# Products of zeros on TensorE: out of the attention loop, into the first maxima

## The chip, the cores and the metric

The kernel runs on one core of a Trainium2 chip. The metric is the device time of the one launch, in microseconds, from the first to the last instruction with what lies around them.

## The reference

One macaron block on `x` of 4 batches x 512 tokens x 128 features: half a mixture-of-experts layer, gated attention with 16 heads of 8 features, and half a mixture-of-experts layer again.

```python
x = x + 0.5 * ffn(layernorm(x), gate_w, Wg, Wu, Wd)      # 8 experts, each takes its 128 best tokens
x = x + attn(layernorm(x), ...)
x = x + 0.5 * ffn(layernorm(x), gate_w, Wg, Wu, Wd)

# attn, for each batch and head
aperture, expression = sigmoid(x @ Wa + ba), sigmoid(x @ We + be)
attn = softmax((x @ Wi) @ (x @ Wo).T / sqrt(8)) * aperture[:, None] * expression[None, :]
attn = attn / (attn.sum(-1) + 1e-8)
out  = rotate_and_scale(attn @ (x @ Wv)) @ Wout
```

The change touches the attention part alone.

## The kernel before

All engines run programs written out by hand and meet at semaphores. The attention part has 16 *steps*: 4 batches by 4 groups `g` of 4 heads. `n` counts them. The queries and keys of a group stand in `q_stack` and `k_stack`, four heads in four blocks of 32 rows, of which a head uses 24 (three parts of its 8 features), and in the scores a 25th row that carries the negative maximum. A step does, for its 4 heads by 4 chunks of 128 tokens:

- 16 units of **maxima**, two steps ahead of use: PE makes a 128 x 512 block of products (`max_scores`, L1120) in one of a ring of three PSUM banks, and DVE reduces it to a negative maximum per row (`take_max`, L794), which raises `max_taken` and so frees the bank. The maxima of a step are turned on PE (`turn_max`, L1128), copied by ACT (L555) and stored as a row of `q_stack` by a DMA of SP.
- 16 units of **scores** in another ring of three banks: PE (`scores`, L1136), then the exponential on ACT (L584) into `probs`.
- 4 **product groups** (`products`, L1150), one for each chunk `c`: four f32 products of `probs` with the values, for the four heads side by side in bank 6, each 2 records in the profile. They wait until ACT has made the chunk's four exponentials. Ahead of the groups of `c` = 1, 2 and 3 stand `KEEP_BUSY` = 6 products of zeros (L1148), 128 rows by 128 columns by 512, f16, which add nothing to bank 6.
- The sums are copied by ACT (L576), turned on PE (`turn_heads`, L1159) and divided on DVE (`norm_heads`, from L860).

PE's order in a step is in `attend`: for `k` = 0 to 7 a unit of scores, one of maxima, one of scores, then what hangs at this `k` (`turn_max` at 0, the last product group of the step before at 1, `turn_heads` at 4, product groups of `c` = 0, 1, 2 at 3, 5, 7), and one of maxima. The last two steps have no maxima; in their place PE turns and projects batches that are done (`turn_combined`, L1220; `project_out`, L1228). Step 0 has no product group at `k` = 1.

Ahead of step 0 the maxima of steps 0 and 1 are made by `first_maxima`, 32 units, with the projections of the last batch between them (`project_qk(3)`, L1087, behind unit 3 of step 0, and `project_vae(3)`, L1100, amid step 1), and in DVE's queue the work that belongs to them; behind the last maxima DVE makes the gates (from L848) before it takes the maxima of step 0's loop.

```python
pe.wait_ge(xnT_ready[1], B)
first_maxima(0, range(RING))
project_qk(3)
first_maxima(0, range(RING, MAX_UNITS))
pe.wait_ge(vae_ready, 2 * 3)
turn_max(0, 0, None)
first_maxima(1, range(MAX_UNITS // 2))
project_vae(3)
first_maxima(1, range(MAX_UNITS // 2, MAX_UNITS))
```

Of the kernel before, what the change touches and what calls it, by code (L numbers as in the profile page):

```python
# [11 lines left out]
P = 128  # L12
# [35 lines left out]
def macaron_block(nc, x_in, Wa, ba, We, be, Wi, Wo, Wv, Wout, chi, beta_p, iv_p, ov_p, gate_w, Wg, Wu, Wd, out):  # L48
# [3 lines left out]
    E, _, I = Wg.shape  # L52
    K = max(1, int(S / E * 2))
    C = S // P
# [12 lines left out]
    with ExitStack() as ctx:  # L67
        def sb(name, shape, dt=F32):
            return ctx.enter_context(nc.sbuf_tensor(name, shape, dt))

        def sem(name):
            return ctx.enter_context(nc.semaphore(name))
# [3 lines left out]
        zeros = sb("zeros", [P, S], F16)  # L76
# [97 lines left out]
        ps = ctx.enter_context(nc.psum_tensor("ps", [P, 8, 512], F32))  # L174
# [53 lines left out]
        max_taken = sem("max_taken")  # L228
# [17 lines left out]

        MAX_UNITS = HG * C
        EXP_UNITS = C * HG
        KEEP_BUSY = 6
        STACK_DMAS = 2 * HG * 16  # L250

        def ring_bank(step, u):


            return (MAX_UNITS * step + u) % RING

        def max_unit(u):

            return u // HG, (u + 2) % HG

        def ring_wait(n, step, u, first_step):


            return n * MAX_UNITS + (u + 1 + (RING - 1 if step == first_step and u == 0 else 0))
# [668 lines left out]
        def _(pe):  # L933
            def chunk(c):
                return slice(c * P, (c + 1) * P)
# [178 lines left out]
            def max_scores(n, step, u):  # L1114

                g = step % G
                qt, j = max_unit(u)
                rows = slice(32 * j, 32 * j + ROWS)
                pe.wait_ge(max_taken, ring_wait(n, step, u, 3))
                nc.tensor.matmul(ps[:, ring_bank(step, u), :], q_stack[rows, g, chunk(qt)], k_stack[rows, g, :],  # L1120
                                 start=True, stop=True).then_inc(max_scores_ready, 1)
# [17 lines left out]
            def products(n, g, c):  # L1139

                pe.wait_ge(probs_ready, n * EXP_UNITS + (HG * c + HG + RING))
                if c == 0:
                    pe.wait_ge(values_ready, 2 * n + 2)
                    pe.wait_ge(heads_copied, n + 1)
                else:

                    for _ in range(KEEP_BUSY):
                        nc.tensor.matmul(ps[:, 6, :], zeros[:, 0:P], zeros[:], start=False, stop=False, skip_group_check=True)  # L1148
                for j in range(HG):
                    last = nc.tensor.matmul(ps[32 * j:32 * j + 32, 6, :], v_ext[:, g, c, j, :], probs[:, c, j, :],  # L1150
                                            start=(c == 0), stop=(c == C - 1), skip_group_check=True)
                last.then_inc(probs_used, 1)

            def turn_heads(n, g, rows):
# [7 lines left out]
            def attend(b, step, first=False, last_batch=False):  # L1162
# [7 lines left out]
                for k in range(MAX_UNITS // 2):  # L1170

                    scores(n, step, 2 * k)
                    if has_max:
                        max_scores(n + 2, step + 2, 2 * k)
                    scores(n, step, 2 * k + 1)
                    if k == 0 and has_next:
                        turn_max(n + 1, (g + 1) % G, None if first else n)
                    if last_batch and step > 1:

                        done = 2 * (step - 2) + k // 4  # L1180
                        if k % 4 == 0 and done < B - 1:
                            turn_combined(done)
                        if k % 4 == 2 and done < B - 1:
                            project_out(done)
                    if k == 1 and not first:
                        products(n - 1, (g - 1) % G, C - 1)
                    if k in (3, 5, 7):
                        products(n, g, k // 2 - 1)
                    if not first and k == TURN_AT:
                        turn_heads(n - 1, g - 1, n + (2 if has_next else 1))  # L1190
                    if has_max:
                        max_scores(n + 2, step + 2, 2 * k + 1)

            def first_maxima(n, units):
                pe.wait_ge(stacks_loaded[n], STACK_DMAS)
                for u in units:
                    max_scores(n, n, u)

            pe.wait_ge(xnT_ready[1], B)
# [8 lines that stand above are left out]
# [23 lines left out]
            for step in range(1, G):  # L1231
                attend(B - 1, step, last_batch=True)
            products(B * G - 1, G - 1, C - 1)
            turn_heads(B * G - 1, G - 1, B * G)
            turn_xn(2, 0)
# [41 lines left out]
```

## Time and profile before

| | |
|---|---|
| median of 3 runs | 559.98 us (557.52 to 560.18) |
| the profiled execution | 560.48 us |
| its span, first to last instruction | 558.8 us |
| mean granted clock of TensorE | 0.931 of full speed |
| PE busy | 456.7 us, 82% of the span |
| DVE busy | 388.1 us, 69% |
| ACT busy | 239.2 us, 43% |
| POOL busy | 56.1 us, 10% |
| DMA, mean over the span | 39 GB/s |

PE's busy time is counted from records of matmuls whose ends are modelled, and weight loads (PEld) run beside them. The granted clock is 1.00 for 2.4 GHz and 0.50 for 1.2 GHz; a stretch that holds a change of the clock shows a value between.

### The profile page before, as it was taken

How to read it: one execution, taken by the hardware profiler on the slowest of the kernel's cores; microseconds unless marked ns; L12 is line 12 of the kernel's file. 1: busy time of each engine (PE TensorE's matmuls, PEld its weight loads, DVE VectorE, ACT ScalarE, POOL GpSimd, SP SyncE). 2: the span in 40 equal slices, each digit the busy share in tenths (PEclk: the TensorE clock that was granted, in tenths of full speed). 3: DMA queues.
4: the chain of work that ended last, by engine and by line, in shares of the span. 5: the costliest groups of instructions: out<-in, count | busy, mean ns of one | idle time of the engine just before them, and what ended most of it. 6: DMA issues, size and time to landing. Idle time of an engine off the chain costs nothing.

```text
span 558.8 us, 8505 instructions
## 1 busy us (share of the span) xinstructions
PE 456.7 (82%) x2540; PEld 225.6 (40%) x2540; DVE 388.1 (69%) x841; ACT 239.2 (43%) x439; POOL 56.1 (10%) x103
## 2 busy tenths in 40 slices
PE   3407999996988989898889898988999711999995
PEld 2402567763443233333233232332343510456773
DVE  6689578878987376766667676766542678948884
ACT  2302533334215355656556565655556210453331
POOL 5700011200001000000000000000000430001210
PEclk9999999998855799999999999999999855899999
DMA  5000011103670110011111000110010000001102
GB/s 153 1 0 1 1 57 56 56 1 113 194 259 1 30 28 19 15 30 29 29 29 28 24 9 25 29 29 1 1 58 1 0 0 2 1 28 58 56 28 75
DMA packets 23146, 21.73 MB, mean 39 GB/s; under 512 B 4113, under 2 KB 16913, under 8 KB 23121
## 3 DMA queue, kind: packets, MB, share of 16 engines
q1 hardware_dynamic: 23120, 21.42, 12.9%
q8 instruction: 13, 0.21, 0.2%
q14 instruction: 13, 0.10, 0.1%
HBM read 13.93 MB, written 7.34 MB: 38 GB/s over the span
## 4 chain that ended last, share of the span: by engine, by line
PE 65%; DVE 20%; issue 11%; ACT 1%; POOL 1%; DMA 1%; DVEq 0%; POOLq 0%; ACTq 0%
PE ps L1148 12%; PE ps L1150 12%; PE ps L1120 11%; DVE neg_max L794 8%; PE ps L1022 4%; DVE probs L733 3%; PE ps L1136 3%; PE ps L1005 2%; PE ps L1037 2%; PE ps L1007 2%; PE ps L1038 2%; PE ps L1006 2%; PE ps L947 2%; PE ps L1159 2%; PE ps L1128 2%
## 5 line engine op out<-in xcount | busy, mean ns | idle before, releaser
L794 DVE TENSOR_REDUCE neg_max<-ps 128x1 f32<-128x512 f32 x256 | 163.4, 684 | 83.3 <-PE ps L1120 83.3
L584 ACT ACTIVATE probs<-ps 128x512 f32<-128x512 f32 x256 | 137.9, 598 | 96.5 <-PE ps L1136 95.5
L1120 PE MATMUL ps<-k_stack,q_stack 24*128 24x512 f32 x256 | 77.2, 537 | 21.0 <-DVE neg_max L794 20.6
L1136 PE MATMUL ps<-q_stack,k_stack 25*128 25x512 f32 x256 | 87.8, 466 | 0.7 <-ACT probs L584 0.7
L1148 PE MATMUL ps<-zeros 128*128 128x512 f16 x288 | 72.9, 391 | 0.0
L1150 PE MATMUL ps<-probs,v_ext 128*32 128x512 f32 x512 | 70.4, 623 | 0.0
L1120 PEld LDWEIGHTS ps<-k_stack,q_stack 24*128 24x128 f32 x256 | 30.0, 196 | 99.1 <-DVE neg_max L794 64.2
L510 ACT CAST picked<-ps 128x512 fp32r<-128x512 f32 x32 | 17.2, 589 | 67.7 <-PE ps L986 67.7
L1148 PEld LDWEIGHTS ps<-zeros 128*128 128x128 f16 x288 | 24.7, 99 | 39.5 <-issue 9.9
L1136 PEld LDWEIGHTS ps<-q_stack,k_stack 25*128 25x128 f32 x256 | 34.8, 190 | 7.9 <-issue 4.0
L733 DVE TENSOR_TENSOR probs<-slot_row,slot 128x1024 f16<-128x1024 f16 x32 | 36.5, 1223 | 0.1
L756 DVE TENSOR_TENSOR vae_and_gates<-heads_out,ps 128x512 f32<-128x512 f32 x32 | 21.9, 687 | 21.0 <-ACT heads_out L518 19.0
L437 POOL TENSOR_TENSOR w_lo<-w_gu,w_hi 128x512 fp32r<-128x512 f32 x16 | 20.7, 1299 | 149.8 <-ACT w_hi L497 149.8
L986 PE MATMUL ps<-probs,xn_hi 128*128 128x512 f16 x64 | 26.7, 417 | 7.3 <-DVE probs L733 6.7
L463 POOL TENSOR_TENSOR v_ext<-vae_and_gates,expression 128x128 f32 (+1 forms) x16 | 6.5, 405 | 251.9 <-PE ps L1150 192.7
L1022 PE MATMUL ps<-vae_and_gates,wd_sb 128*128 128x512 f32 x64 | 30.5, 599 | 0.8 <-DVE vae_and_gates L756 0.8
L1005 PE MATMUL ps<-picked,w_hi 128*128 (+1 forms) x64 | 30.1, 470 | 1.1 <-ACT picked L510 0.8
L522 ACT COPY down_out<-ps 128x512 f32<-128x512 f32 x16 | 9.4, 587 | 44.0 <-PE ps L1022 44.0
L961 PE MATMUL ps<-ident,threshold_row 32*128 32x32 f32 x2 | 0.6, 311 | 33.4 <-DVE threshold_row L703 33.4
L986 PE MATMUL ps<-probs,xn_lo 128*128 128x512 f16 x64 | 26.6, 416 | 0.0
L518 ACT ACTIVATE heads_out<-ps 128x512 f32<-128x512 f32 x32 | 19.1, 598 | 15.5 <-PE ps L1007 13.7
L1007 PE MATMUL ps<-picked,w_lo 128*128 (+1 forms) x64 | 25.2, 394 | 0.0
(157 smaller groups left out, 608.8 us busy)
## 6 DMA issues: line engine op xcount, KB each, us to landing
parts_dram<-part_hi SPq DMA_DIRECT2D x8, 512.0 KB, 3.3
q_stack<-parts_dram SPq DMA_DIRECT2D x64, 48.0 KB
k_stack<-parts_dram SPq DMA_DIRECT2D x64, 48.0 KB
w_gu<-in_L_ffn_Wg_dram SPq DMA_DIRECT2D x16, 128.0 KB, 2.1
w_gu<-in_L_ffn_Wu_dram SPq DMA_DIRECT2D x16, 128.0 KB, 2.2
wd_sb<-in_L_ffn_Wd_dram SPq DMA_DIRECT2D x16, 128.0 KB, 2.4
parts_dram<-part_lo SPq DMA_DIRECT2D x8, 256.0 KB, 3.9
x<-in_L_attn_x_dram SPq DMA_DIRECT2D x4, 256.0 KB, 3.6
```

The source lines that it names most:

```text
L584: nc.scalar.activation(probs[:, u // HG, u % HG, :], ps[:, RING + ring_bank(step, u), :], ACT.Exp, scale=SCORE_SCALE).then_inc(probs_ready, 1)
L733: nc.vector.tensor_tensor(pick[:, b, c], slot_row[:].unsqueeze(1).broadcast_to([P, E, K]), slot[:, c, b * E:(b + 1) * E].unsqueeze(2).broa ...
L756: nc.vector.tensor_tensor(hidden[:, u, m, :], silu[:, m, :], ps[:, 5 - m, :], ALU.mult).then_inc(hidden_ready[l], 1)
L794: nc.vector.tensor_reduce(neg_max[:, g, qt, j:j + 1], ps[:, ring_bank(step, u), :], AX.X, ALU.max, negate=True).then_inc(max_taken, 1)
L986: last = nc.tensor.matmul(ps[:, pick_bank(n) + k, :], half[:, C * b + c, :], pick[:, b, c, 4 * hf:4 * hf + 4, :], start=(c == 0), stop=(c ...
L1005: nc.tensor.matmul(ps[:, bank, :], w_hi[:, u, k, cols], tokens_hi, start=True, stop=False)
L1007: nc.tensor.matmul(ps[:, bank, :], w_lo[:, u, k, cols], tokens_hi, start=False, stop=True).then_inc(gate_up_done[l], 1)
L1022: last = nc.tensor.matmul(ps[:, 6, :], wd_sb[:, u, m, :], hidden[:, u, m, :], start=(m == 0), stop=(m == MI - 1))
L1120: nc.tensor.matmul(ps[:, ring_bank(step, u), :], q_stack[rows, g, chunk(qt)], k_stack[rows, g, :], start=True, stop=True).then_inc(max_sco ...
L1136: nc.tensor.matmul(ps[:, RING + ring_bank(step, u), :], k_stack[rows, g, chunk(c)], q_stack[rows, g, :], start=True, stop=True).then_inc(s ...
L1148: nc.tensor.matmul(ps[:, 6, :], zeros[:, 0:P], zeros[:], start=False, stop=False, skip_group_check=True)
L1150: last = nc.tensor.matmul(ps[32 * j:32 * j + 32, 6, :], v_ext[:, g, c, j, :], probs[:, c, j, :], start=(c == 0), stop=(c == C - 1), skip_g ...
```

## The change

The products of zeros in `products` are taken out. In `first_maxima` three of them are put ahead of every second unit, into the bank that this unit's maxima will overwrite, behind the wait for that bank: 8 times in each of the two steps, 48 products, where the loop had 288.

```diff
-        KEEP_BUSY = 6
+        KEEP_BUSY = 3
...
                 if c == 0:
                     pe.wait_ge(values_ready, 2 * n + 2)
                     pe.wait_ge(heads_copied, n + 1)
-                else:
-
-                    for _ in range(KEEP_BUSY):
-                        nc.tensor.matmul(ps[:, 6, :], zeros[:, 0:P], zeros[:], start=False, stop=False, skip_group_check=True)
                 for j in range(HG):
                     last = nc.tensor.matmul(ps[32 * j:32 * j + 32, 6, :], v_ext[:, g, c, j, :], probs[:, c, j, :],
-                                            start=(c == 0), stop=(c == C - 1), skip_group_check=True)
+                                            start=(c == 0), stop=(c == C - 1))
...
             def first_maxima(n, units):
                 pe.wait_ge(stacks_loaded[n], STACK_DMAS)
                 for u in units:
+                    if u % 2 == 0:
+                        pe.wait_ge(max_taken, ring_wait(n, n, u, 3))
+                        for _ in range(KEEP_BUSY):
+                            nc.tensor.matmul(ps[:, ring_bank(n, u), :], zeros[:, 0:P], zeros[:], start=True, stop=True)
                     max_scores(n, n, u)
```

## Rows read from the trace of the kernel before

**Rows 1.** The page: the span, the chain by engine, two costliest groups.

```profile
span 558.8 us, 8505 instructions
...
PE 65%; DVE 20%; issue 11%; ACT 1%; POOL 1%; DMA 1%; DVEq 0%; POOLq 0%; ACTq 0%
...
L794 DVE TENSOR_REDUCE neg_max<-ps 128x1 f32<-128x512 f32 x256 | 163.4, 684 | 83.3 <-PE ps L1120 83.3
...
L1148 PE MATMUL ps<-zeros 128*128 128x512 f16 x288 | 72.9, 391 | 0.0
```

**Rows 2.** Timeline, one step; start, us, engine, line, out<-in, count, wait.

```profile
302.41 1.06 PE L1150 MATMUL ps<-probs,v_ext 128*32 128x512 f32 x8
...
305.87 1.47 PE L1148 MATMUL ps<-zeros 128*128 128x512 f16 x6
...
307.26 1.06 PE L1150 MATMUL ps<-probs,v_ext 128*32 128x512 f32 x8
...
309.97 1.07 PE L1150 MATMUL ps<-probs,v_ext 128*32 128x512 f32 x8
...
312.88 1.47 PE L1148 MATMUL ps<-zeros 128*128 128x512 f16 x6
...
314.28 1.06 PE L1150 MATMUL ps<-probs,v_ext 128*32 128x512 f32 x8
...
316.99 1.47 PE L1148 MATMUL ps<-zeros 128*128 128x512 f16 x6
```

**Rows 3.** Instructions of line 860 from 196 to 400 us.

```profile
L860 DVE TENSOR_TENSOR den_a<-ps,z_weight x13: 164/166/166, 199.8 to 393.9; 128x16 f32<-128x16 f32 x13
```

**Rows 4.** Stretches; length, busy PE, PEld, DVE, ACT, POOL, clock, DMA share, GB/s.

```profile
147.29:150.44 3.15, 2.57 (x8) 1.01 (x7) 3.15 (x6) 0.58 (x1) 0.00 (x0) 1.00 0.55 156
150.44:168.08 17.64, 14.99 (x35) 7.68 (x36) 15.66 (x27) 2.49 (x3) 0.00 (x0) 0.50 0.66 226
168.08:175.17 7.09, 5.86 (x21) 2.52 (x21) 7.02 (x12) 4.28 (x8) 2.06 (x8) 0.50 0.01 2
175.17:177.03 1.86, 1.86 (x10) 0.20 (x8) 1.02 (x2) 0.73 (x2) 0.00 (x0) 0.50 0.00 0
177.03:179.33 2.30, 1.95 (x12) 0.79 (x9) 1.47 (x3) 1.43 (x3) 0.00 (x0) 0.50 0.00 0
...
184.57:188.26 3.69, 3.15 (x23) 0.85 (x17) 2.48 (x4) 2.06 (x4) 0.00 (x0) 1.00 0.17 33
188.26:191.25 2.99, 2.21 (x17) 1.00 (x13) 1.52 (x3) 1.29 (x3) 0.00 (x0) 1.00 0.32 91
191.25:194.81 3.56, 3.56 (x15) 0.90 (x14) 1.15 (x2) 1.44 (x3) 0.00 (x0) 0.52 0.03 7
194.81:401.00 206.19, 184.88 (x1155) 64.76 (x1147) 134.90 (x256) 120.33 (x229) 6.71 (x24) 1.00 0.08 22
401.00:434.60 33.60, 32.38 (x195) 13.37 (x192) 11.58 (x44) 20.50 (x39) 0.75 (x2) 1.00 0.08 25
```

**Rows 5.** Timeline of PE at the low clock, from 155 us.

```profile
161.47 2.50 PE L1100 MATMUL ps<-wvae_sb,xnT 128*128 128x160 f32 x8
...
169.66 1.01 PE L1128 MATMUL ps<-ident,neg_max 128*4 128x128 f32 x4 [0.40 <-DVE neg_max L794]
...
178.61 0.79 PE L1120 MATMUL ps<-k_stack,q_stack 24*128 24x512 f32 x1 [0.35 <-DVE neg_max L794]
...
179.33 2.74 PE L1148 MATMUL ps<-zeros 128*128 128x512 f16 x6
182.00 1.94 PE L1150 MATMUL ps<-probs,v_ext 128*32 128x512 f32 x8
```

**Rows 6.** One stretch, PE alone: length, busy, clock, DMA share, GB/s.

```profile
308.26:312.88 4.62, 4.08 (x32) 1.00 0.00 0
```

**Rows 7.** Timeline of DVE around the first maxima.

```profile
145.98 9.71 DVE L794 TENSOR_REDUCE neg_max<-ps 128x1 f32<-128x512 f32 x16
...
169.97 1.75 DVE L850 RECIPROCAL expression<-vae_and_gates 128x256 f32<-128x256 f32 x1
```

## The prediction

> **What bounds the kernel now.** I read the page first: the chain of work that ended last is PE for 65% and DVE for 20%, and the costliest groups are the maxima (L794, DVE, 256 of 684 ns) and, on PE, 288 products of zeros at 391 ns each, 72.9 us of busy time [rows 1]. The page's clock row dips near 150 us and is at full speed through most of the loop. Then I went to the attention loop in order of time [rows 2]. Some words for it: a *pair* is one product of scores (L1136) and one of maxima (L1120); a *product group* is the 8 matmul records of L1150 behind one chunk `c`; a *zeros group* is the six products at L1148 ahead of three of the four product groups of a step.
>
> At full clock a zeros group holds PE 1.39 us (305.87 to 307.26) and a product group 1.00 us (307.26 to 308.26, where the next stretch begins). Between product groups lie four pairs: 1.71 us (308.26 to 309.97), 1.91 us where the heads are turned (310.97 to 312.88), 1.71 us again (315.28, when the product group of 314.28 is done, to 316.99), and 2.47 us across the step's seam, where the maxima are turned (303.41 to 305.87) [rows 2]. The sum, 7.8 + 4.0 + 3 x 1.39 = 16.0 us, is the step: the first op of each heads norm (L860) comes 13 times from 199.8 to 393.9 us, so 194.1 / 12 = 16.17 us a step, once in four steps with a longer seam [rows 3]. PE is busy 184.88 of the 206.19 us from 194.81 to 401.00, DVE 134.90, ACT 120.33, the DMA engines 8% [rows 4]. So PE sets the pace, and a quarter of what it does are zeros. Whether they can go depends on PE's clock.
>
> **The clock, as these rows show it.** The two levels are 1.2 and 2.4 GHz; the granted clock reads 0.50 or 1.00.
> - It fell at 150.44 after 3.15 us in which PE ran mainly products of maxima, busy 2.57 of 3.15 by the record. It stayed at 0.50 through 17.64 us of maxima with projections among them, busy 14.99, then through the first 7.09 us of step 0 [rows 4].
> - It did not come back for a product group (175.17 to 177.03) with five pairs ahead of it and four behind it (177.03 to 179.33) [rows 4]. It didn't for a stretch of 2.50 us of dense f32 projections (161.47) between maxima either. It came back at 184.57, after six zeros in a row and a product group in a row (179.33 to 183.87) [rows 4, 5].
> - It fell again at 191.40, after the seam of 188.26 to 191.25, where PE had four pairs and a turn of the maxima, busy 2.21 of 2.99, and no product group [rows 4].
> - At 308.26 to 312.88 no zeros ran, only one product group, eight pairs and a turn of the heads, and the clock stayed at 1.00 [rows 6].
>
> So pairs, which use 24 or 25 of the array's 128 rows, hardly count as work for the clock; a product group now and then keeps a fast clock, but does not bring one back, and the zeros do.
>
> **The change part by part.** (a) *48 zeros in the first maxima, three ahead of every second unit of steps 0 and 1.* The maxima there are paced by DVE: 16 units in 9.71 us, 0.607 us each [rows 7]. Three zeros cost 3 x 0.233 = 0.70 us (1.39 / 6 each), and two maxima about 0.5 us at full clock, against 1.21 us that DVE needs for two; so they fit in the steady part, and keep the clock up there. At both ends they don't: the first two groups come ahead of `project_qk(3)`, which holds PE two microseconds more before unit 3, and the ring of three holds DVE only 1.8 us; I estimate +1.5 us, from +0.3 at the start of step 1, +0.5 at its unit 8, +1.7 at step 0, less 1.0 for the projection of 161.47, which takes 2.50 us at the low clock and half at the high one [rows 5]. Bounds 0 and +3. The new wait at `max_taken` is the one that the maxima product behind it has anyway; behind it on PE stand the next scores and projections. SP's stores of the fourth batch start that much later, and are first read in the loop, several steps on.
>
> (b) *Step 0.* The maxima's last zeros end near 166.5 us. Then DVE has the gates to make: a reciprocal of 1.75 us at 169.97 with small ops around it, so that it takes maxima again only from about 171.9 [rows 7], and four of them must be taken before the first product group, so that the first product group can't come much before the 175.17 of now [rows 4]. That is some 8 us of pairs alone, waiting for DVE at either clock; by what happened at 147.29 to 150.44 and 188.26 to 191.25, the clock falls there. From then on step 0 is as now at the low clock, without 2.67 us (179.33 to 182.00) and 1.40 us of zeros, but with the last product group 0.87 and the last pairs 0.3 slower: -2.9 us. Bounds -3.5 and -2.
>
> (c) *Steps 1 to 13 without zeros.* Does the clock come back? Each step would be four times the pattern of 175.17 to 179.33, a product group amid pairs, and that one did not bring it back. I take it that it stays at 1.2 GHz. At that clock a product group takes 1.86 us (175.17 to 177.03) and the four pairs between two groups 2.30 us (177.03 to 179.33) [rows 4], of which 0.35 is a wait for DVE that remains: the ring is empty after each group [rows 5]. The turn of the heads adds 0.95 but fills that wait: 2.8. The seam: the turn of the maxima can start when the last maximum is taken, 0.79 + 0.68 + some 0.1 us after its product was issued, takes 0.95, and three more pairs without wait and a score, about 0.95: 3.5 [rows 1, 5]. Sum 4 x 1.86 + 2.3 + 2.3 + 2.8 + 3.5 = 18.3, with the longer seam (+0.6) in one of four 18.5 us. Against 13 x 16.17 + 1.6 (step 1 runs partly at the low clock now, 191.25 to 194.81 [rows 4]) = 211.8, that is 13 x 18.5 = 240.5: **+28 us**. Bounds: every pair at DVE's 0.6 us and both turns in full, 9.6 + 7.4 + 2.0 + 0.5 = 19.5, +42; both turns wholly hidden, 17.9, +21.
>
> (d) *Steps 14 and 15*, 401.00 to 434.60, have no maxima, and PE is busy 32.38 of 33.60 us [rows 4]: what goes is gained, what slows is lost. Seven zeros groups go, 9.8 us. The 23.8 left grow: nine product groups by 0.87 (7.8), 30 scores, 512 columns long as the zeros, by 0.21 (2.67 / 6 less 1.39 / 6; 6.4), three `project_out`, three `turn_combined` and two turns of heads by some 5: +9.5 us if the clock stays low throughout. Here dense projections stand beside the product groups, so it may come back midway; I take +7, bounds -3 and +10. (e) The transposes and projections behind the loop at the low clock: +1, bounds 0 and +2. (f) `skip_group_check` and the other constants issue nothing: 0, and nothing is hidden. The transfers of a step are 8% of the DMA engines' time, and a longer step gives them more room.
>
> Sum: 1.5 - 2.9 + 28 + 7 + 1 = +34.6 us on the profiled execution's 560.48 (span 558.8 and 1.7 around it); the median of the runs, 559.98, is 0.5 below that. **About 595 us.**
>
> **Rivals.** *The clock holds: faster.* If pairs and product groups keep the clock at 2.4 GHz, as they did at 308.26 to 312.88 [rows 6], or the loop's product groups bring it back, each of 13 steps loses three zeros groups less a little more waiting for DVE (16 maxima at 0.607 are 9.7 us, norms 0.7): about -4.0, -52 in all; step 0 at full clock -7.4, step 1's dip -1.6, steps 14 and 15 -9, first maxima +1.5: 560.5 - 68.5 = 492 us. It decides from the first product group that raises the clock. Against it: 175.17 to 179.33 didn't, the seam loses it (188.26), and a seam without product groups comes in every step. This rival is also what the Trainium skill would have: the page "TensorE: Matmul & The Clock Gate", section "Why this matters for your kernels", says that the clock drops mid-kernel after idle gaps between bursts of matmuls, and to avoid those. No such gap stands in the loop, where PE is busy 184.88 of 206.19 us, so by that rule the zeros are for nothing; the fall at 150.44, with PE busy by the record, speaks against it.
>
> *The clock comes and goes* with how its changes fall on the pattern, half of the loop at each level: between 515 and 575, say 545 us. *It is low from the start:* if it falls among the first maxima, the zeros are a burden there: 3 x 0.445 (2.67 / 6) and two maxima as long, 2.2 us for two units against 1.21, 16 times, +15 us, so 610 us. The rows of 179.33 show how zeros last at the low clock [rows 5]; against it stands that a mix without any zeros held the clock at 308.26 to 312.88 [rows 6].
>
> **Numbers.** My forecast 70%, low from the start 12%, coming and going 10%, holding 8%. The likeliest one's bounds are 560.5 + 14.5 = 575 and 560.5 + 55 = 615. The range 572 to 613 leaves out the fast case, most of the mixed one, and the far end of the slow ones. A measurement of this kernel tells 0.5% (2.8 us) from no change. Faster: 8 + 6 = 14%; same 2%; slower 84%.
>
> **What the profile after would show.** Right: a granted clock of 1.00 during the first maxima, 0.50 from about 170 us to at least 400 us, product groups at 1.9 us, steps of 18 to 19 us, no wait of DVE behind zeros, PE's busy share in the loop about as high as now. Wrong: a clock at 1.00 in the loop and steps near 12 us (the product groups alone keep or restore it), or a clock low already at 150 us. If the clock is low and the step nonetheless near 16 us, my pairs are too dear.

## The result, and the profile after

The changed kernel takes 593.49 us (median of 4 runs, 592.84 to 594.04) against 558.91 before (4 runs): a ratio of 1.062, 95% interval 1.058 to 1.065. It is slower by 6%, and the forecast was 595. The profiled execution took 594.04 us; its span is 592.3. Medians are over all runs of a kernel; the ratios with intervals, here and below, are of its faster runs, and differ from those of the medians by up to 0.8%.

From the page of the changed kernel, the lines that answer to [rows 1], with PE's busy share, the clock row (40 slices, tenths of full speed) and the product groups (now L1146):

```profile
span 592.3 us, 8025 instructions
...
PE 496.8 (84%) x2300; PEld 228.1 (39%) x2300; DVE 390.5 (66%) x841; ACT 241.8 (41%) x439; POOL 56.3 (9%) x103
...
PEclk9999999999995555555555555555558965699999
...
PE 70%; DVE 16%; issue 10%; ACT 2%; POOL 1%; DMA 1%; DVEq 0%; POOLq 0%; ACTq 0%
...
L1146 PE MATMUL ps<-probs,v_ext 128*32 128x512 f32 x512 | 116.9, 1004 | 0.0
```

PE has 240 products fewer and is busy 40 us longer. Its share is about what it was; only the clock row tells why. The stretches of the changed kernel (length, busy PE, PEld, DVE, ACT, POOL, granted clock, DMA share, GB/s), which answer to [rows 4]:

```profile
145.21:170.68 25.47, 23.66 (x99) 9.35 (x96) 21.68 (x37) 3.66 (x5) 0.00 (x0) 1.00 0.62 213
170.68:175.04 4.36, 2.10 (x13) 0.85 (x11) 4.29 (x7) 2.63 (x5) 0.10 (x1) 1.00 0.00 0
175.04:187.91 12.87, 12.00 (x48) 3.32 (x49) 8.66 (x15) 6.73 (x12) 1.96 (x8) 0.50 0.04 8
187.91:439.94 252.03, 236.57 (x940) 72.23 (x936) 139.86 (x260) 125.56 (x234) 6.77 (x24) 0.50 0.07 19
439.94:448.10 8.16, 7.80 (x34) 3.95 (x31) 1.38 (x2) 4.30 (x8) 0.00 (x0) 0.50 0.14 37
448.10:467.40 19.30, 18.70 (x125) 7.86 (x124) 8.89 (x37) 15.34 (x28) 0.00 (x0) 1.00 0.10 27
467.40:592.30 124.90, 90.78 (x513) 60.68 (x509) 92.74 (x195) 36.65 (x65) 19.93 (x26) 0.86 0.10 28
```

The zeros keep the clock up through the first maxima (first row). Step 0 begins at 170.68 and waits for DVE's gates, and the clock falls 4.36 us into it, with PE busy 2.10 us of these. It falls in the longest of the waits, the one that ends here:

```profile
175.21 0.79 PE L1120 MATMUL ps<-k_stack,q_stack 24*128 24x512 f32 x1 [1.73 <-DVE neg_max L794]
```

The clock stays at 1.2 GHz for 273 us, through all of steps 1 to 13, and comes back at 448.10, in step 14. Cut at the same points of the program, the two kernels compare like this:

| stretch | before | after | difference | forecast |
|---|---|---|---|---|
| ahead of the first maxima | 144.94 | 145.21 | +0.3 | |
| first maxima | 23.14 | 25.47 | +2.3 | +1.5 |
| step 0 | 20.18 | 17.23 | -2.9 | -2.9 |
| steps 1 to 13 | 212.28 | 252.03 | +39.8 | +28 |
| steps 14 and 15 | 34.00 | 27.46 | -6.5 | +7 |
| the rest | 124.26 | 124.90 | +0.6 | +1 |
| span | 558.8 | 592.3 | +33.5 | +34.6 |

One step of the changed kernel, from the timeline of PE (the answer to [rows 2]):

```profile
289.02 1.94 PE L1146 MATMUL ps<-probs,v_ext 128*32 128x512 f32 x8
...
293.26 1.94 PE L1146 MATMUL ps<-probs,v_ext 128*32 128x512 f32 x8
295.13 0.79 PE L1120 MATMUL ps<-k_stack,q_stack 24*128 24x512 f32 x1
...
296.28 1.11 PE L1155 MATMUL ps<-ident,heads_out 128*128 128x128 f32 x4
297.32 0.79 PE L1120 MATMUL ps<-k_stack,q_stack 24*128 24x512 f32 x1
...
298.47 1.94 PE L1146 MATMUL ps<-probs,v_ext 128*32 128x512 f32 x8
...
302.71 1.94 PE L1146 MATMUL ps<-probs,v_ext 128*32 128x512 f32 x8
...
306.15 1.01 PE L1128 MATMUL ps<-ident,neg_max 128*4 128x128 f32 x4 [0.36 <-DVE neg_max L794]
...
308.24 1.94 PE L1146 MATMUL ps<-probs,v_ext 128*32 128x512 f32 x8
```

A product group holds PE 1.87 us (293.26 to 295.13). From one to the next are 4.24, 5.21, 4.24 and 5.53 us, 19.2 in all. Two pairs take 1.15 us here (295.13 to 296.28).

### The profile page after: what moved, and what is told of

Same layout as the page of the kernel before. It is cut to its first block, busy times and chain, and to the rows that moved or that the text cites. A ratio compares the mean times of both kernels' runs of the same rounds, so it can differ in the third digit from the quotient of the medians.

```text
span 592.3 us, 8025 instructions
## 1 busy us (share of the span) xinstructions
PE 496.8 (84%) x2300; PEld 228.1 (39%) x2300; DVE 390.5 (66%) x841; ACT 241.8 (41%) x439; POOL 56.3 (9%) x103
## 4 chain that ended last, share of the span: by engine, by line
PE 70%; DVE 16%; issue 10%; ACT 2%; POOL 1%; DMA 1%; DVEq 0%; POOLq 0%; ACTq 0%
PE ps L1146 19%; PE ps L1120 16%; DVE neg_max L794 7%; PE ps L1136 4%; PE ps L1022 4%; PE ps L1155 3%; PE ps L1128 2%; PE ps L986 2%; PE ps L1005 2%; PE ps L1037 2%; PE ps L1007 2%; PE ps L1038 2%; PE ps L1006 2%; PE ps L947 2%; DVE xn L625 1%
## 5 line engine op out<-in xcount | busy, mean ns | idle before, releaser
L584 ACT ACTIVATE probs<-ps 128x512 f32<-128x512 f32 x256 | 139.4, 595 | 135.3 <-PE ps L1136 135.1
L1136 PE MATMUL ps<-q_stack,k_stack 25*128 25x512 f32 x256 | 134.6, 685 | 0.6 <-ACT probs L584 0.6
L1146 PE MATMUL ps<-probs,v_ext 128*32 128x512 f32 x512 | 116.9, 1004 | 0.0
L1120 PE MATMUL ps<-k_stack,q_stack 24*128 24x512 f32 x256 | 102.8, 751 | 14.7 <-DVE neg_max L794 14.7
L1120 PEld LDWEIGHTS ps<-k_stack,q_stack 24*128 24x128 f32 x256 | 37.9, 269 | 147.6 <-DVE neg_max L794 141.6
L1136 PEld LDWEIGHTS ps<-q_stack,k_stack 25*128 25x128 f32 x256 | 53.5, 290 | 8.8 <-ACT probs L584 6.8
L1005 PE MATMUL ps<-picked,w_hi 128*128 (+1 forms) x64 | 30.4, 474 | 1.1 <-ACT picked L510 0.8
L518 ACT ACTIVATE heads_out<-ps 128x512 f32<-128x512 f32 x32 | 19.2, 599 | 15.2 <-PE ps L1007 13.4
L1146 PEld LDWEIGHTS ps<-probs,v_ext 128*32 128x32 f32 x512 | 12.5, 136 | 32.6 <-issue 23.1
L1006 PE MATMUL ps<-picked,w_hi 128*128 (+1 forms) x64 | 25.1, 391 | 0.0
```

The lines of the kernel that those rows point to most:

```text
L584: nc.scalar.activation(probs[:, u // HG, u % HG, :], ps[:, RING + ring_bank(step, u), :], ACT.Exp, scale=SCORE_SCALE).then_inc(probs_ready, 1)
L1005: nc.tensor.matmul(ps[:, bank, :], w_hi[:, u, k, cols], tokens_hi, start=True, stop=False)
L1006: nc.tensor.matmul(ps[:, bank, :], w_hi[:, u, k, cols], tokens_lo, start=False, stop=False)
L1136: nc.tensor.matmul(ps[:, RING + ring_bank(step, u), :], k_stack[rows, g, chunk(c)], q_stack[rows, g, :], start=True, stop=True).then_inc(s ...
```

## The experiments

The theory: pairs alone lose the fast clock, a product group amid pairs does not bring it back, and zeros with a product group behind them do. So the zeros of the loop are what costs 34 us to take away, and the moved ones are worth nothing. Rivals: the moved zeros do the harm or some good; the loop would hold a clock that it once had. Times are medians where no single ones are given, each beside runs of the kernel before on the same chip.

### The two halves of the change

`no_zeros`: the kernel before, with the loop's zeros taken out and nothing added.

```diff
-                else:
-
-                    for _ in range(KEEP_BUSY):
-                        nc.tensor.matmul(ps[:, 6, :], zeros[:, 0:P], zeros[:], start=False, stop=False, skip_group_check=True)
```

> The kernel before without the 288 zeros of the loop and without zeros in the first maxima: one half of the change alone. My theory (the loop cannot bring the clock back from 1.2 GHz): the clock falls near 150 us as before, stays low to the last two steps, steps 1 to 13 take 19.4 us each as in the changed kernel, and only the 2.2 us that the zeros cost in the first maxima are gone: 591 us (589 to 593). Rival (the zeros in the first maxima are what hurts, or the clock holds by itself once they are gone): 500 to 560 us.

593.21 us, ratio 1.060 (1.053 to 1.068): the 34 us of the change belong to this half. The clock fell at 151.0 and came back at 447.9 us. I had expected 591 us (589 to 593), with the 2.2 us of the first maxima gone. In the trace they are gone, and most of them is lost again at the end: the first maxima take 23.12 us against the changed kernel's 25.47, steps 1 to 13 take 252.04 against 252.03, but the clock comes back 10.4 us into step 14 and not 8.2, and steps 14 and 15 take 28.43 against 27.46, the rest 125.67 against 124.90.

`both`: the kernel before, all its zeros kept, with three zeros more ahead of every second unit of the first maxima.

```diff
                 for u in units:
+                    if u % 2 == 0:
+                        pe.wait_ge(max_taken, ring_wait(n, n, u, 3))
+                        for _ in range(3):
+                            nc.tensor.matmul(ps[:, ring_bank(n, u), :], zeros[:, 0:P], zeros[:], start=True, stop=True)
                     max_scores(n, n, u)
```

> The kernel before with three zeros ahead of every second unit of the first maxima as well: the other half of the change alone, all 288 zeros of the loop kept. My theory: the first maxima are paced by DVE at either clock and the clock falls in step 0 anyway, so that the added zeros cost their 2.2 us and give nothing back: 561 us (558 to 563). Rival (a clock kept up into step 0 is worth its 5 to 7 us there, and the loop's zeros then keep it): 553 us.

561.46 us against 559.58 for the kernel before, ratio 1.003 (0.998 to 1.008): no difference that can be told. In the trace the added zeros cost what they did in the changed kernel: the first maxima take 26.01 us against 23.14, with the clock at 1.00 for all but 3.4 us of them, and steps 1 to 13 take the same 212.28. So the other half costs 2 to 3 us, which the medians can't tell from nothing, and gives nothing back.

### Does a fast clock hold in a loop without zeros?

`burst0`: the changed kernel with 48 zeros more in step 0, which carry the clock into the loop.

```diff
                 for k in range(MAX_UNITS // 2):
-
+                    if first:
+                        busy(6, k < 4)      # six zeros into bank 6
                     scores(n, step, 2 * k)
```

> The changed kernel with six more zeros at each of the eight k of step 0, into bank 6, so that the clock is high when step 0 ends; no zeros in steps 1 to 15. My theory: it is lost at a seam of one of the first steps, where 2.5 to 3 us pass without a product group, and never comes back before step 14; each step run high gains some 7 us, so 560 to 592 us. Rival (product groups and pairs hold a clock that is once high): high to the end, steps of 12.3 us, 500 to 505 us.

Its four single times were 581.66, 581.59, 539.09 and 569.33 us, at mean clocks of 0.774, 0.774, 0.866 and 0.796. Three lie in my range of 560 to 592, the fastest below it. Stretches of the profiled execution:

```profile
192.00:215.70 23.70, 21.30 (x142) 8.31 (x143) 20.89 (x41) 18.37 (x37) 1.12 (x4) 1.00 0.12 31
215.70:437.50 221.80, 208.88 (x829) 64.87 (x826) 120.76 (x230) 110.65 (x207) 5.61 (x20) 0.50 0.08 21
```

Up to 215.70 the loop ran at 2.4 GHz without a single zero, and its step was 12.1 us, by the heads norm:

```profile
L860 DVE TENSOR_TENSOR den_a<-ps,z_weight x2: 165/165/165, 198.2 to 210.3; 128x16 f32<-128x16 f32 x2
```

That is the price of the rival that the prediction named (16.17 - 4.0). But the clock was lost at the third seam behind the burst, that of step 3. The timeline of PE there:

```profile
213.20 1.06 PE L1146 MATMUL ps<-probs,v_ext 128*32 128x512 f32 x8
214.20 0.50 PE L1120 MATMUL ps<-k_stack,q_stack 24*128 24x512 f32 x1
...
215.48 0.87 PE L1128 MATMUL ps<-ident,neg_max 128*4 128x128 f32 x4 [0.55 <-DVE neg_max L794]
216.28 0.79 PE L1120 MATMUL ps<-k_stack,q_stack 24*128 24x512 f32 x1
```

Maxima of 0.50 us before it, of 0.79 behind it, and no return for 222 us. So both halves of the theory stand here: a fast clock can be held for some steps, and once lost in this loop, without zeros, it is lost until step 14. The scatter of the single runs, with their mean clocks, fits a fall in another step each time, which is not shown: only the profiled one shows its step.

`burst0_seam3` adds three zeros where PE waits at the seam.

```diff
+                    if k == 0 and not first:
+                        busy(3)
                     if k == 0 and has_next:
                         turn_max(n + 1, (g + 1) % G, None if first else n)
```

> The kernel of the burst in step 0 with three zeros at the seam of every later step, ahead of the turn of the maxima, where PE waits for DVE. My theory (only the seam loses the clock, product groups hold it elsewhere): granted clock 1.00 from step 0 to the end of the loop, steps of 12.4 to 12.8 us, 505 to 515 us. Rival (a loop with one quarter of the zeros is too thin anywhere): the clock falls as in the changed kernel, 590 to 600 us.

503.19, 543.34, 543.70 and 577.65 us. The best run, with a mean clock of 0.951, is probably what the loop gives when the clock holds nearly throughout; it has no profile. The profiled one held it for eight steps, from 190 to 289.70:

```profile
190.00:289.70 99.70, 92.17 (x604) 36.17 (x604) 85.19 (x161) 74.77 (x145) 4.48 (x16) 1.00 0.13 34
289.70:395.50 105.80, 101.50 (x392) 31.91 (x395) 54.57 (x101) 49.57 (x93) 2.23 (x8) 0.50 0.05 14
```

It fell again at a seam, just ahead of the three zeros (they start at 289.68), and three zeros a step did not bring it back for 106 us, until step 14. My expectation of 505 to 515 us failed: three runs lie far above it, and the fastest just below. With the clock held, the three zeros cost nothing (12.0 to 12.1 us a step, as in `burst0`), and they do not keep the clock from falling. Whether they make a fall rarer four runs do not settle.

### How many zeros, and where?

`half`: the kernel before with three zeros in each place instead of six.

```diff
-        KEEP_BUSY = 6
+        KEEP_BUSY = 3
```

> The kernel before with three zeros instead of six ahead of each of three product groups, nothing in the first maxima: 144 products of zeros. My theory: the loop still has stretches dense enough (three zeros and a product group in a row) to bring the clock back after a fall, so it is high for nearly all of the loop, a step takes 16.2 - 3 x 0.70 = 14.1 us, and the whole 525 to 535 us. Rival (less than six zeros cannot bring it back): after the fall at 150 us it stays low and the zeros only add to the changed kernel: above 600 us.

534.45 us, ratio 0.958 (0.952 to 0.964). In the profiled execution the clock was low from 148.1 to 206.1 us, came back in the loop, and stayed to 417.7, behind the loop. Half the zeros were surplus.

`c3_only`: the kernel of `burst0`, with six zeros ahead of the last product group of a step alone (`k` = 1 of the next, behind the seam).

```diff
+                if c == C - 1:
+                    busy(6)
                 for j in range(HG):
```

> The kernel of the burst in step 0 with six zeros ahead of the last product group of a step alone (96 in the loop). My theory: falls happen at a seam, and the six zeros with the product group behind them bring the clock back within a step or two, which the three zeros of the seam could not: steps of 13.4 us with a dip now and then, 515 to 535 us, and little spread between runs. Rival (a fall is for good, as in the two kernels with a burst): single runs anywhere from 510 to 590 us.

526.85 us, ratio 0.947 (0.942 to 0.952), single runs from 519.9 to 531.3: falls are now repaired. The profiled execution had one in the loop, at 246.7, over after 3.4 us. `even8` and `even14` spread the zeros instead, on top of `burst0`, where I thought PE had time to spare.

```diff
+                    else:
+                        busy({1: 1, 4: 1, 5: 1, 6: 1, 7: 1}.get(k, 0))     # even14: {1: 2, 4: 1, 5: 2, 6: 1, 7: 2}
...
+                    if k == 0 and not first:
+                        busy(3)                                            # even14: 6
```

> The kernel of the burst in step 0 with eight zeros a step, three ahead of the turn of the maxima and one at each of k = 1, 4, 5, 6, 7, where PE waits for DVE at times. My theory: what counts is that no few microseconds pass with one product group alone; the clock stays at 1.00 to the end of the loop in nearly all runs, part of the zeros lies in PE's waits: 505 to 515 us. Rival (only long dense stretches hold it): it falls in some step and stays low, single runs spread to 590 us.

> The same with fourteen zeros a step, six ahead of the turn of the maxima and 2, 1, 2, 1, 2 at k = 1, 4, 5, 6, 7. My theory: the clock holds in every run, at 1.4 us a step less what PE's waits hide: 515 to 530 us, slower than eight a step by 8 to 18 us if that one holds. Rival: as for eight.

`even8`: 551.60, 561.14, 593.99 and 612.51 us; `even14`: 561.94 us (median of 10, 553.4 to 571.7), ratio 1.000 (0.996 to 1.004), by the medians 1.008. Both expectations failed. In `even8` it was first the clock: in the slowest run, the profiled one, it fell at the seam of step 1 (191.2), stayed low for 171 us with PE busy 167.43 of 170.67, and fell once more. But it was not the clock alone: `even14` had it at 1.00 from 219.9 to 445.2 us in the profiled execution, and still its step took 15.8 us in that time (157.7 us for ten), against 16.17 with eighteen zeros in rows [rows 3]. The timeline of PE at a single zero in `even14`:

```profile
240.34 0.49 PE L1120 MATMUL ps<-k_stack,q_stack 24*128 24x512 f32 x1
240.76 0.39 PE L1160 MATMUL ps<-zeros 128*128 128x512 f16 x1
241.08 0.50 PE L1136 MATMUL ps<-q_stack,k_stack 25*128 25x512 f32 x1
241.08 0.49 PE L1120 MATMUL ps<-k_stack,q_stack 24*128 24x512 f32 x1
241.09 0.49 PE L1136 MATMUL ps<-q_stack,k_stack 25*128 25x512 f32 x1
```

The products of scores and maxima start together, within 0.01 us, as at 241.08, when nothing of full height stands between them. A zero does: it starts 0.42 us behind the maximum at 240.34, and the next pair 0.32 us behind it, 0.74 us from one maximum to the next. Without it a pair takes 0.33 us in a row of pairs. A zero dropped among the pairs costs more than its 0.233 us in a row of six. The steps at 2.4 GHz say how much (from one L860 to the next): 12.0 to 12.1 us in `burst0_seam3`, and 14.5 in `even8`, which has the same and five single zeros more, 0.48 us each. Six in a row, in `c3_only`, make it 13.2 to 13.3, 0.2 us each.

`even14` also has the one fall in steps 1 to 13 of any of these runs that is not at a seam or just behind it: at 202.83, ten microseconds into step 1, amid pairs, one product group and one zero, with PE hardly waiting. The stretch before it, PE alone:

```profile
198.88:202.83 3.95, 3.86 (x25) 1.00 0.01 2
```

So a wait of PE is not needed to lose the clock.

`c1_only`: `c3_only` with the six zeros ahead of the second product group (`c == 1`, `k` = 5) in place of the last.

> The kernel with first maxima and burst, but the six zeros ahead of the second product group of a step (k = 5) in place of the last: same count, another place. My theory: the seam, with no zeros on either side of it, loses the clock more often, and the six bring it back within a step: 530 to 550 us with more spread than at the last group. Rival (the place makes no difference): 520 to 531 us.

573.29 us, single runs from 547.7 to 592.9. Stretches of the profiled execution, between changes of the clock:

```profile
198.00:232.90 34.90, 31.13 (x202) 11.38 (x199) 27.26 (x54) 23.30 (x46) 1.12 (x4) 1.00 0.10 28
232.90:249.90 17.00, 16.58 (x64) 5.19 (x64) 7.47 (x16) 6.92 (x14) 0.56 (x2) 0.50 0.06 19
249.90:253.40 3.50, 2.36 (x16) 0.73 (x14) 3.28 (x6) 2.66 (x5) 0.00 (x0) 0.99 0.14 38
253.40:270.40 17.00, 16.65 (x64) 5.24 (x66) 7.46 (x14) 7.04 (x13) 0.56 (x2) 0.50 0.06 16
270.40:287.50 17.10, 14.87 (x98) 5.35 (x98) 13.72 (x26) 11.70 (x23) 0.56 (x2) 1.00 0.11 29
```

Six zeros at `k` = 5 raise the clock, and a seam soon takes it away: it fell at 232.90 and 253.40, both at a seam, and came back 17 us later. The place makes the difference, by 46 us in the medians, which was more than I expected (530 to 550); the fastest run here is 16 us above the slowest of `c3_only`. The mean clock here is 0.84, and 0.96 in the profiled execution of `c3_only`.

### What is the least that works?

`c3_no_first` is `c3_only` without the zeros in the first maxima.

> Six zeros ahead of the last product group of a step, the burst in step 0, and none in the first maxima: what the 48 moved zeros are worth. My theory: nothing, since the burst in step 0 raises the clock anyway; their 2.2 us go: 1 to 4 us below the same kernel with them (526.9), 522 to 527 us. Rival (a clock held through the first maxima is needed): slower than with them, 530 us or more.

526.93 us, with them 526.85 (each beside its own runs of the kernel before: 0.943 and 0.947, with overlapping intervals). The zeros that the change moved there are worth nothing here either.

`c3_and_c1` adds three zeros ahead of the second product group to that.

```diff
-                if c == C - 1:
-                    busy(6)
+                if c == C - 1 or (c == 1):
+                    busy(6 if c == C - 1 else 3)
```

> Six zeros ahead of the last product group and three ahead of the second, the burst in step 0, none in the first maxima. My theory: the three cost 0.70 us a step, 10 us in all, and save most of the dips at the low clock that the kernel with six alone still shows: 520 to 530 us with less spread. Rival (dips come at the seam alone, so three zeros at k = 5 only cost): 533 to 537 us.

538.86 us, ratio 0.960 (0.954 to 0.966): 12 us more than without them. The profiled execution still dipped at 249.7, 307.7 and 365.8, 3.4 us each. The rival was right, the three only cost, and the spread (534 to 543) was no smaller.

`c3_alone`: the kernel before with its six zeros kept ahead of the last product group only, no burst, nothing in the first maxima.

```diff
                 if c == 0:
...
-                else:
+                elif c == C - 1:
```

> The kernel before with its six zeros kept ahead of the last product group alone, neither burst nor first maxima: 96 zeros in all. My theory: the clock, low from 150 us, is brought back by the six zeros of one of the steps 1 to 5, each step run low costing some 8 us; 530 to 550 us. Rival (one dense stretch a step is too rare to bring it back): near 600 us.

**525.33 us, ratio 0.938 (0.933 to 0.943)**, single runs from 520.6 to 526.9: the fastest median of all, 6% under the kernel before and 11% under the changed one, by one condition in the kernel before. It is also below my 530 to 550, since the clock came back in the first step that could bring it. It does what the change wanted, by a third of the zeros. Stretches of its profiled execution:

```profile
149.30:193.70 44.40, 38.91 (x125) 15.15 (x126) 31.58 (x52) 14.68 (x26) 2.06 (x8) 0.50 0.29 100
193.70:244.90 51.20, 45.02 (x299) 16.52 (x300) 41.33 (x79) 36.60 (x70) 2.25 (x8) 1.00 0.12 31
244.90:248.30 3.40, 3.40 (x14) 0.79 (x12) 0.96 (x2) 1.24 (x3) 0.00 (x0) 0.50 0.11 28
```

The clock is low through step 0, comes back at the first six zeros of step 1, and is lost in four seams for 3.4 to 6.8 us each (from 244.90, 258.50, 302.90 and 316.55). One of these, by the timeline of PE:

```profile
301.85 0.60 PE L1128 MATMUL ps<-ident,neg_max 128*4 128x128 f32 x4
...
303.12 2.74 PE L1148 MATMUL ps<-zeros 128*128 128x512 f16 x6
305.79 1.30 PE L1150 MATMUL ps<-probs,v_ext 128*32 128x512 f32 x8
307.01 0.49 PE L1120 MATMUL ps<-k_stack,q_stack 24*128 24x512 f32 x1
```

The seam loses the clock, the zeros run at half speed (2.74 us for six), the product group is half through when the clock is back (1.30 us, between 1.06 and 1.94), and the pairs behind it are fast again. A fall is over after 3.4 to 6.8 us where the zeros stand right behind the seam, and mostly after 17 us where they stand two product groups later (`c1_only`).

## Why the prediction was right

The mechanism held. That the total came so close, 593.5 against 595, is luck: two terms were off in opposite directions, by +11.8 and -13.5 us.

- **The clock.** It was at 1.00 during the first maxima, fell in step 0 and stayed low through steps 1 to 13, as read from 175.17 to 179.33 and from 188.26 [rows 4]. `burst0` and the two halves show that this, and not the moved zeros, is the cause: the rival that the clock holds had its price right (12.1 us a step at 2.4 GHz) and its condition wrong.
- **(a) First maxima**, +2.3 for +1.5: DVE waited 1.64 us for unit 3 behind `project_qk(3)`, as described. `both` has the same cost in its trace, +2.9.
- **(b) Step 0**, -2.9 for -2.9. The first maxima's last zeros ended at 170.3 us, not near 166.5, but the wait for the gates and the fall in it came as described.
- **(c) Steps 1 to 13** is the first mis-sized term: +39.8 for +28. A step took 19.4 us (252.03 / 13), not 18.5. The product groups were right (1.87), and so nearly were the two plain gaps (2.37 each for 2.30). The turn of the heads was not: I let it fill a wait for DVE and gave its gap 2.8 us (my own terms, 2.30 + 0.95 - 0.35, make 2.9), and it took 3.34 (295.13 to 298.47), two pairs in front of it and two behind it at 1.15 us each, and the turn's 1.04 in full. Split in two twos, the pairs hold PE longer than the 2.30 less 0.35 that I had left for four in a row, and there was no wait to fill. The seam took 3.66 for 3.5. The measured step lies inside the bounds, 17.9 to 19.5, near the upper one, which priced every pair at 0.6.
- **(d) Steps 14 and 15** is the second: -6.5 for +7, outside its bounds of -3 and +10. The step that failed is when the clock comes back, and what that is worth. It came 8.16 us into the 27.46, behind the product group of 444.04 and the first projection (446.62). And +7 did not even fit the "midway" that I gave for it: half of the 19.2 us by which the work grows, less the 9.8 of the zeros, is about 0. That the dense f32 products did here what zeros do elsewhere is likely and not shown: these steps have no maxima either, and no run separates the two. From then on the loop without zeros is simply the shorter one.
- **The rule of the Trainium skill** that spoke against me, in "TensorE: Matmul & The Clock Gate", section "Why this matters for your kernels" (idle gaps between bursts lose the clock), does not explain the loop: PE was busy 236.57 of 252.03 us in steps 1 to 13 and at half its clock in all of them. It may bear on the falls, most of which come where PE waits: it was busy 2.10 of the 4.36 us before the fall of the changed kernel. But the fall of `even14` came with PE busy 3.86 of 3.95 us.

Still open: what exactly loses the clock. In most falls looked at, at a seam or in step 0, narrow products and waits of PE come together (1.73 us in the changed kernel, 0.55 at the seam of `burst0`). The fall of `even14` shows that a busy PE can lose it too; no run shows what waits would do without the narrow products, or whether the number of rows is what counts in these. Open too is why single runs of `burst0`, `burst0_seam3` and `even8` fall in different steps. The code is the same and the seam comes in every step, so something that is not in the program seems to decide at which seam it happens; no run here isolates it. It was not tried to fill the seam itself with real products instead of zeros.

## What to carry to other kernels

Before you take "useless" matmuls away, look at the granted clock with and without them: a busy PE is no sign of a fast one, and the same loop took 12.1 us or 19.4 us a step. Work that keeps a clock and work that brings it back are different: find the place where it is lost (here mostly the seam of a step, with narrow products and a wait) and put one dense stretch right behind it, joined to other dense work, rather than a little everywhere. And check a loop that "sometimes" runs fast over several runs: one good profile of a kernel whose clock can fall for good tells little about its median.

## What was not expected of the hardware

- The clock can stay at either level over the same work. The same loop without zeros held 2.4 GHz from 192.00 to 215.70 us (`burst0`), and stayed at 1.2 GHz for the 222 us behind it.
- A busy PE neither keeps the clock (3.86 of 3.95 us before the fall of `even14`) nor brings it back: it was busy 94 to 98% in long stretches at 0.50 (252.03 us in the changed kernel, 170.67 in `even8`). Most products there use 24 or 25 of 128 rows, which is the likely reason; no run changes the rows alone.
- A full-height product between two narrow ones on different row blocks ends their common start: 0.74 us for one pair and one zero, against 0.33 for a pair and 0.233 for a zero in a row of six.
